# Exchanging transposed blocks of an attention kernel through memory instead of between partitions

## The chip, the cores and the metric

The kernel runs on one core of a Trainium2 chip. The metric is the device time of one execution in microseconds (us). The engines are TensorE (PE in the profile, its weight loads PEld), VectorE (DVE), ScalarE (ACT), GpSimd (POOL) and SyncE (SP), which here only issues transfers. Sixteen DMA engines carry them out. A tile lies in SBUF over 128 partitions.

## What is computed

The input x is (4, 128, 32, 32): four batches, 128 channels, 1024 positions. Cut to what matters, the reference is:

```python
N = H * W                                             # 1024
xg = x.reshape(B, 4, C // 4, H, W)                     # four groups of channels
y = (xg - mu) * rsqrt(var + EPS) * gn_gamma + gn_beta
q, k, v = split(einsum('bchw,dc->bdhw', y, w_qkv) + b_qkv, 3, axis=1)
scores = einsum('bnc,bcm->bnm', q, k) * C ** (-0.5)
w = softmax(scores, axis=-1)
a = einsum('bnm,bmc->bnc', w, v)
out = einsum('bchw,dc->bdhw', a, w_out) + b_out
return x + out
```

Everything is float32.

## The kernel before, in words

The two projections of queries and keys are folded into one matrix, and so are those of the values and of the output: per batch there is y (normalised input), z (y times the folded matrix) and v (values, the output matrix already in them). The scores are z times y, held in pairs of a head and a tail part (hi, lo) and multiplied in three passes.

The queries are worked in 32 blocks of 128, n = 0 to 31, eight per batch. One step of the program (a slot) handles one block on each engine. Four blocks are a group: eight groups, 0 to 7, of 512 queries each. For a block the order is: TensorE writes its scores (128 queries by 1024 keys, lines 778 to 781) two slots ahead; VectorE takes the maximum (line 577); ScalarE the exponential into `probs`, a ring of four blocks (line 426); then the block must be transposed, since the product with the values sums over the keys, which must lie on the partitions.

Group 0 and the last group are transposed on TensorE (`turn`, line 798). For groups 1 to 6 (`SWAPPED`) this is done in two steps. VectorE transposes within squares of 32 by 32 (`flip(n)`, line 605), issued one slot ahead of its block. A square is then right in itself but sits on the wrong 32 partitions. SyncE exchanges the squares (`swap(group)`, line 255) when all four blocks of the group are flipped: 16 transfers of 32 partitions by 4 KB, each from `flipped` on partitions 32g to `home` on partitions 32t. There are two tiles `flipped` and two `home`, used by even and odd groups in turn.

TensorE multiplies the home of a group with the values (`mix`, line 833), eight key tiles k of two passes each. The table `MIX` sets when: two tiles in each of the slots 4 group + 7 to 4 group + 10, that is, from four slots after the last flip of the group has been issued. Group 6 gets two tiles in slot 31 and the other six after the loop, then the last group follows. Before the first tile TensorE waits for all transfers of the group. VectorE then scales the product by the inverse row sums (`scale`, line 615), GpSimd adds the input (line 333), SyncE stores the result (line 265).

SyncE issues in the order of its program, one queue for all: for a group its inverse row sums to memory (`keep_rows`, line 238), the 16 swaps, the sums back, spread over all partitions (`spread_rows` into `inv_wide`, line 245), and the result of two groups before. Its waits hold all that stands behind them. A flip of groups 3 to 6 waits for the swaps of two groups before; a swap of these groups waits for the mix of two groups before.

Which transfer waits for which is said in its first lines:

```python
def swap(group):
    sp.wait_ge(s_flipped, QB * group)
    if group > 2:
        sp.wait_ge(s_mixed, KT * (group - 1))
```

Of the kernel before, what the change touches and what calls it, by code (L numbers as in the profile page):

```python
# [5 lines left out]
def attention_kernel(nc, x, vectors, weights, out):  # L6
# [36 lines left out]
    GROUP = QB * N  # L43
    GROUPS_OF_FOUR = BATCHES * HALVES
# [3 lines left out]
    SWAP = 16 * SQ * SQ  # L48
# [4 lines left out]

    inverse_rows = nc.dram_tensor("inverse_rows", (GROUPS_OF_FOUR - 1, HALF), fp32)

# [4 lines left out]
    with ctx:  # L60
        def sb(name, shape, dt=fp32):
            return ctx.enter_context(nc.sbuf_tensor(name, shape, dt))
# [58 lines left out]
        flipped_even = sb("flipped_even", [128, GROUP])  # L121
        with nc.sbuf_tensor("flipped_odd", [128, GROUP], fp32) as flipped_odd:
            pass
        last_head = sb("last_turned_head", [128, KT, HALF], fp32r)
        flipped = (flipped_even, flipped_odd)
        home = sb("home_even", [128, GROUP]), sb("home_odd", [128, GROUP])
# [63 lines left out]
        s_swapped = [sem("squares_swapped_even"), sem("squares_swapped_odd")]  # L190
# [24 lines left out]
        def swaps(group):  # L215

            return SWAP * len([g for g in SWAPPED if g <= group and g % 2 == group % 2])

# [8 lines left out]
        def _(sp):  # L227
# [20 lines left out]
            def swap(group):  # L248
                sp.wait_ge(s_flipped, QB * group)
                if group > 2:  # L250
                    sp.wait_ge(s_mixed, KT * (group - 1))
                for k in range(SQ):
                    for g in (0, 2, 1, 3):
                        t = g ^ k
                        sp.dma_start(home[group % 2][32 * t:32 * t + 32, g * N:(g + 1) * N],  # L255
                                     flipped[group % 2][32 * g:32 * g + 32, t * N:(t + 1) * N]
                                     ).then_inc(s_swapped[group % 2], 16)
# [11 lines left out]
            for group in SWAPPED:  # L269
                keep_rows(group)  # L270
                swap(group)
                spread_rows(group)
                if group >= 2:
                    store(group - 2)
# [114 lines left out]
        def _(act):  # L389
# [39 lines left out]
            def turned_copy(n):  # L429
                act.wait_ge(s_turned, 2 * turns(n) + 1)  # L430
                if n < QB:
                    act.activation(copy_of_turned(first_turned, n, 0), turned_tiles(0), ACT.Copy).then_inc(s_copied[0], 1)
                    return
                act.wait_ge(s_swapped[1], swaps(5))
                for j in range(2):
                    act.wait_ge(s_turned, 2 * turns(n) + j + 1)
                    act.activation(copy_of_turned(last_head, n, j), turned_tiles(j), ACT.Copy).then_inc(s_turned_hi, 1)
# [55 lines left out]
        def _(dve):  # L493
# [106 lines left out]
            def flip(n):  # L600
                group, u = n // QB, n % QB
                dve.wait_ge(s_exp, n + 1)
                if group > 2:
                    dve.wait_ge(s_swapped[group % 2], swaps(group - 2))
                dve.transpose(flipped[group % 2][:, :].rearrange("p (tv u c) -> p tv u c", u=QB, c=32)[:, :, u, :],  # L605
                              probs[:, n % RING, :].rearrange("p (v t r) -> p t v r", t=SQ, r=32)
                              ).then_inc(s_flipped, 1)
# [99 lines left out]
        def _(pe):  # L707
# [96 lines left out]
            def mix(group, count):  # L804
                b, g = group // HALVES, group % HALVES
                bank = mixed[:, g, :]
                for k in range(tiles_mixed[group], tiles_mixed[group] + count):
                    if k == 0:
# [11 lines left out]
                        if group in SWAPPED:  # L820
                            pe.wait_ge(s_swapped[g], swaps(group))
# [9 lines left out]
                    else:  # L831
                        there = home[g][:, :].rearrange("p (g v u c) -> p v u g c", g=SQ, v=KT, u=QB)[:, k, :, :, :]
# [120 lines left out]
```

## Time and profile before

| | us |
|---|---|
| median of 3 runs | 137.71 (137.03 to 138.33) |
| the profiled execution | 138.07 |
| its span in the profile | 136.3 |
| TensorE busy | 129.4 (95%) |
| VectorE busy | 99.8 (73%) |
| ScalarE busy | 65.0 (48%) |
| GpSimd busy | 41.4 (30%) |

The busy shares say which engine has room. The waits name who stood idle until whom. The chain follows what ended last back to its causes. A timeline lists instructions with their start and duration; for a transfer that is the time that SyncE took to issue it, and its landing is shown apart. A window's row gives for a stretch the busy time of each engine, the granted TensorE clock as a share of full speed, the mean busy share of the DMA engines and their GB/s.

### The profile page before, as it was taken

Reading aid. Unit: us, or ns where it says so; the run is one execution under the profiler, and the core shown is the slowest. Engines: PE = TensorE matmul, PEld = TensorE weight load, DVE = VectorE, ACT = ScalarE, POOL = GpSimd, SP = SyncE. Lnnn points to the kernel's source line nnn. Section 1 sums busy time; section 2 is a strip of 40 time slices with the busy share of each in tenths; the row PEclk is TensorE's granted clock in tenths of the full one; section 3 lists DMA queues with packets and bytes.
Section 4 is the critical chain, followed back from the end, with each engine's and each line's share of the span. In section 5 each row is a group of like instructions: output and inputs, shape, how many; then the busy total and the mean of one; then the engine's idle time right before and its main releaser. Section 6 shows DMA issues by size and latency. Waiting matters only on the chain.

```text
span 136.3 us, 1759 instructions
## 1 busy us (share of the span) xinstructions
PE 129.4 (95%) x543; PEld 89.1 (65%) x543; DVE 99.8 (73%) x170; ACT 65.0 (48%) x117; POOL 41.4 (30%) x49
## 2 busy tenths in 40 slices
PE   6999999998999949999999999999999999999990
PEld 6987688875777526666666666666656577554670
DVE  0589699999998996877686889866868886761302
ACT  3154778854675372544542475544633474730000
POOL 6032130730022229300190058000770367303210
PEclk9999999999999999999999999999999999999999
DMA  4940000030056978985689656888888459961011
GB/s 152 350 191 0 0 5 0 3 77 0 0 111 147 210 188 236 207 203 169 154 204 206 204 114 160 191 195 224 203 202 201 122 123 209 209 176 77 0 77 77
DMA packets 8937, 19.01 MB, mean 139 GB/s; under 512 B 3040, under 2 KB 3040, under 8 KB 8928
## 3 DMA queue, kind: packets, MB, share of 16 engines
q1 hardware_dynamic: 8640, 18.63, 53.8%
q10 hardware_dynamic: 288, 0.27, 0.6%
q8 instruction: 4, 0.07, 0.2%
q14 instruction: 5, 0.04, 0.2%
HBM read 4.20 MB, written 2.11 MB: 46 GB/s over the span
## 4 chain that ended last, share of the span: by engine, by line
PE 75%; DVE 12%; SPq 7%; issue 2%; DMA 2%; DVEq 0%
PE mixed L833 31%; PE scores L778 7%; SPq L255 7%; PE scores L779 7%; PE scores L781 7%; DVE scores L577 5%; PE scores L839 4%; PE turned L798 3%; DVE flipped_odd L605 3%; PE turned L723 3%; DMA home_odd<-flipped_odd 2%; PE mixed L830 1%; PE mixed L828 1%; PE mixed L829 1%; PE mixed L723 1%
## 5 line engine op out<-in xcount | busy, mean ns | idle before, releaser
L577 DVE TENSOR_SCALAR_CACHE_REDUCE scores<-scores,key_bias 128x1024 f32<-128x1024 f32 x31 | 40.0, 1289 | 15.0 <-PE scores L781 14.7
L426 ACT ACTIVATE probs<-scores,neg_max 128x1024 f32<-128x1024 f32 x32 | 35.7, 1116 | 22.7 <-DVE scores L577 21.9
L833 PE MATMUL mixed<-home_odd,v 128*128 128x512 f32 x48 | 22.6, 594 | 1.9 <-DMA home_odd<-flipped_odd 1.9
L833 PE MATMUL mixed<-home_even,v 128*128 128x512 f32 x48 | 22.1, 594 | 0.0
L778 PE MATMUL scores<-y_hi_odd,z_hi_odd 128*128 128x512 f32 x32 | 18.7, 585 | 0.6 <-DVE z_lo_odd L544 0.6
L778 PE MATMUL scores<-y_hi_even,z_hi_even 128*128 128x512 f32 x30 | 15.9, 531 | 0.0
L605 DVE STREAM_TRANSPOSE flipped_odd<-probs 128x1024 f32<-128x1024 f32 x12 | 14.8, 1235 | 0.3 <-DMA home_odd<-flipped_odd 0.3
L605 DVE STREAM_TRANSPOSE flipped_even<-probs 128x1024 f32<-128x1024 f32 x12 | 14.8, 1234 | 0.0
L833 PEld LDWEIGHTS mixed<-home_even,v 128*128 128x128 f32 x48 | 8.9, 189 | 7.8 <-issue 7.2
L833 PEld LDWEIGHTS mixed<-home_odd,v 128*128 128x128 f32 x48 | 8.5, 190 | 8.3 <-issue 8.0
L779 PE MATMUL scores<-y_lo_odd,z_hi_odd 128*128 128x512 f32 x32 | 12.6, 392 | 0.0
L333 POOL TENSOR_TENSOR result<-result,xs 128x512 f32<-128x512 f32 x7 | 8.9, 1278 | 9.9 <-DVE result L615 9.9
L779 PE MATMUL scores<-y_lo_even,z_hi_even 128*128 128x512 f32 x30 | 11.8, 392 | 0.0
L615 DVE TENSOR_TENSOR result<-mixed,inv_wide 128x512 f32<-128x512 f32 x7 | 7.4, 1051 | 4.4 <-PE mixed L833 4.4
L781 PE MATMUL scores<-y_hi_odd,z_lo_odd 128*128 128x512 f32 x32 | 9.9, 391 | 0.0
L778 PEld LDWEIGHTS scores<-y_hi_odd,z_hi_odd 128*128 128x128 f32 x32 | 6.0, 189 | 5.7 <-issue 3.6
L310 POOL TENSOR_TENSOR z_lo_odd<-z_full,z_hi_odd 128x512 fp32r<-128x512 f32 x2 | 2.6, 1300 | 22.3 <-ACT z_full L417 22.3
L781 PE MATMUL scores<-y_hi_even,z_lo_even 128*128 128x512 f32 x30 | 9.3, 392 | 0.0
L305 POOL TENSOR_TENSOR y_lo_odd<-y,y_hi_odd 128x512 fp32r<-128x512 f32 x4 | 5.1, 1289 | 13.6 <-ACT y_hi_odd L395 13.6
L779 PEld LDWEIGHTS scores<-y_lo_odd,z_hi_odd 128*128 128x128 f32 x32 | 6.0, 189 | 4.3 <-issue 3.6
L798 PEld LDWEIGHTS turned<-ident,probs 128*128 128x128 f32 x64 | 7.5, 140 | 1.9 <-issue 1.1
L798 PE MATMUL turned<-ident,probs 128*128 128x128 f32 x64 | 8.3, 272 | 0.0
(162 smaller groups left out, 202.9 us busy)
## 6 DMA issues: line engine op xcount, KB each, us to landing
home_odd<-flipped_odd SPq DMA_DIRECT2D x48, 128.0 KB, 2.4
home_even<-flipped_even SPq DMA_DIRECT2D x48, 128.0 KB, 2.4
out_dram<-result SPq DMA_DIRECT2D x8, 256.0 KB, 3.5
inv_wide<-inverse_rows SPq DMA_DIRECT2D x7, 256.0 KB, 3.6
xs<-in_x_dram SPq DMA_DIRECT2D x2, 512.0 KB, 6.5
xs<-in_x_dram SPq DMA_DIRECT2D x3, 256.0 KB, 4.6
xs<-in_x_dram ACTq DMA_DIRECT2D x1, 256.0 KB, 3.3
ws<-in_weights_dram SPq DMA_DIRECT2D x1, 256.0 KB, 4.0
```

The source lines that it names most:

```text
L255: sp.dma_start(home[group % 2][32 * t:32 * t + 32, g * N:(g + 1) * N], flipped[group % 2][32 * g:32 * g + 32, t * N:(t + 1) * N]).then_inc ...
L333: pool.tensor_tensor(result[:, g, :], result[:, g, :], xs[:, b, g * HALF:(g + 1) * HALF], ALU.add).then_inc(s_result, 1)
L426: act.activation(probs[:, i % RING, :], scores[:, i % 2, :], ACT.Exp, bias=neg_max[:, i:i + 1], scale=-1.0, accum_out=row_sum[:, i:i + 1]) ...
L577: dve.tensor_scalar(scores[:, i % 2, :], scores[:, i % 2, :], key_bias[:, b % 2, i:i + 1], None, ALU.subtract, ALU.min, accum_out=neg_max[ ...
L605: dve.transpose(flipped[group % 2][:, :].rearrange("p (tv u c) -> p tv u c", u=QB, c=32)[:, :, u, :], probs[:, n % RING, :].rearrange("p ( ...
L615: dve.tensor_tensor(result[:, g, :].rearrange("p (u q) -> p u q", u=QB), mixed[:, g, :].rearrange("p (u q) -> p u q", u=QB), inv_wide[:, g ...
L723: mm = pe.matmul(bank[:, (t - lo) * VW:(t - lo) * VW + C + 1], y[:, b % 2, t * 128:(t + 1) * 128], wv_out[:, 0:C + 1], start=True, stop=True)
L778: pe.matmul(to[h], z_hi[b % 2][:, query], y_hi[b % 2][:, halves[h]], start=True, stop=False)
L779: pe.matmul(to[h], z_hi[b % 2][:, query], y_lo[b % 2][:, halves[h]], start=False, stop=False)
L781: mm = pe.matmul(to[h], z_lo[b % 2][:, query], y_hi[b % 2][:, halves[h]], start=False, stop=True)
L798: mm = pe.transpose(turned[:, j, k * 128:(k + 1) * 128], probs[:, n % RING, key:key + 128], ident[:, :])
L833: mm = pe.matmul(bank, v[:, b % 2, k, :], there, start=first, stop=final)
```

## The change

A flipped block no longer goes from partitions to partitions. Each is written to a tensor in memory as soon as it is flipped (`keep`, 512 KB, 128 partitions with four pieces of 1 KB each), and two blocks at a time are read back to their home by four transfers (`bring`, each 256 KB: 32 partitions with four pieces of 2 KB). `flipped` becomes a ring of four blocks, laid out block by block, so the flip writes a contiguous row; `home` becomes three tiles, and the mix reads it in a new order of dimensions. A flip waits for the keep of the block four before (with its partner in the pair); a bring waits for the keeps of its two blocks and, from group 4 on, for the mix of three groups before. The head of the last group's turned blocks takes the place of `home_1` instead of `flipped_odd`, and its copy waits for the mix of groups up to 4.

```diff
-    SWAP = 16 * SQ * SQ
+    SQUARES = 32 * KT
+    HOMES = 3
+    SWAP = 16 * SQ * 2
...
+    squares = nc.dram_tensor("squares", (len(SWAPPED), 2, 128, SQ, 2, SQUARES), fp32)
...
-        flipped_even = sb("flipped_even", [128, GROUP])
-        with nc.sbuf_tensor("flipped_odd", [128, GROUP], fp32) as flipped_odd:
+        flipped = sb("flipped", [128, RING, N])
+        with nc.sbuf_tensor("last_turned_head", [128, KT, HALF], fp32r) as last_head:
             pass
-        last_head = sb("last_turned_head", [128, KT, HALF], fp32r)
-        flipped = (flipped_even, flipped_odd)
-        home = sb("home_even", [128, GROUP]), sb("home_odd", [128, GROUP])
+        home_1 = sb("home_1", [128, GROUP])
+        home = sb("home_0", [128, GROUP]), home_1, sb("home_2", [128, GROUP])
...
+        def pairs_kept(n):
+
+            return 32 * (n // 2 - 1)
...
-            def swap(group):
-                sp.wait_ge(s_flipped, QB * group)
-                if group > 2:
-                    sp.wait_ge(s_mixed, KT * (group - 1))
-                for k in range(SQ):
-                    for g in (0, 2, 1, 3):
-                        t = g ^ k
-                        sp.dma_start(home[group % 2][32 * t:32 * t + 32, g * N:(g + 1) * N],
-                                     flipped[group % 2][32 * g:32 * g + 32, t * N:(t + 1) * N]
-                                     ).then_inc(s_swapped[group % 2], 16)
+            def keep(n):
+                group, u = n // QB, n % QB
+                sp.wait_ge(s_flipped, n - QB + 1)
+                sp.dma_start(squares[group - 1, u // 2, :, :, u % 2, :],
+                             flipped[:, n % RING, :].rearrange("p (t w) -> p t w", t=SQ)).then_inc(s_kept, 16)
+
+            def bring(group, half):
+                sp.wait_ge(s_kept, pairs_kept(QB * group + 2 * half))
+                if half == 0 and group > HOMES:
+                    sp.wait_ge(s_mixed, KT * (group - HOMES + 1))
+                for t in range(SQ):
+                    there = home[group % HOMES][32 * t:32 * t + 32, :].rearrange("p (g w) -> p g w", g=SQ)
+                    sp.dma_start(there[:, :, half * 2 * SQUARES:(half + 1) * 2 * SQUARES],
+                                 squares[group - 1, half, :, t, :, :].rearrange("(g r) u w -> r g (u w)", g=SQ)
+                                 ).then_inc(s_swapped[group % HOMES], 16)
...
             for group in SWAPPED:
+                keep(QB * group)
+                keep(QB * group + 1)
+                bring(group, 0)
+                keep(QB * group + 2)
                 keep_rows(group)
-                swap(group)
+                keep(QB * group + 3)
+                bring(group, 1)
                 spread_rows(group)
...
-                if group > 2:
-                    dve.wait_ge(s_swapped[group % 2], swaps(group - 2))
-                dve.transpose(flipped[group % 2][:, :].rearrange("p (tv u c) -> p tv u c", u=QB, c=32)[:, :, u, :],
+                if group > SWAPPED[0]:
+                    dve.wait_ge(s_kept, pairs_kept(n - RING))
+                dve.transpose(flipped[:, n % RING, :].rearrange("p (t v c) -> p t v c", t=SQ, c=32),
...
-                        there = home[g][:, :].rearrange("p (g v u c) -> p v u g c", g=SQ, v=KT, u=QB)[:, k, :, :, :]
+                        there = home[group % HOMES][:, :].rearrange("p (g u v c) -> p v u g c", g=SQ, u=QB, v=KT)[:, k, :, :, :]
```

The queue of SyncE for group 3 before: its row sums, the 16 swaps, the sums back, the result of group 1.

```order
L238 DMA inverse_rows<-inv_sum 128x4 [waits group_inv_sums_ready]
L255 DMA home_odd<-flipped_odd 32x1024 [waits mixed_tiles_done,squares_flipped]
L255 DMA home_odd<-flipped_odd 32x1024 x15
L245 DMA inv_wide<-inverse_rows 128x512 [waits mixed_scaled,inv_rows_kept_odd]
L265 DMA out_dram<-result 128x512 [waits result_ready]
```

The same place after the change (its own line numbers: 258 is `keep`, 267 is `bring`, 252 and 277 the two old transfers).

```order
L258 DMA squares<-flipped 512x1x256 [waits squares_flipped] x2
L267 DMA home<-squares 32x4x512 [waits squares_kept]
L267 DMA home<-squares 32x4x512 x3
L258 DMA squares<-flipped 512x1x256 [waits squares_flipped]
L245 DMA inverse_rows<-inv_sum 128x4 [waits group_inv_sums_ready]
L258 DMA squares<-flipped 512x1x256 [waits squares_flipped]
L267 DMA home<-squares 32x4x512 [waits squares_kept]
L267 DMA home<-squares 32x4x512 x3
L252 DMA inv_wide<-inverse_rows 128x512 [waits mixed_scaled,inv_rows_kept_odd]
L277 DMA out_dram<-result 128x512 [waits result_ready]
```

One wait in front of 16 transfers has become two waits for landings, each with four brings behind it, and the third and fourth keep of a group stand behind the first half's brings.

VectorE around the first flips of group 3 before (577 is the maximum, 615 the scaling).

```order
L577 TENSOR_SCALAR scores,neg_max<-scores,key_bias 128x1024 [waits scores_ready,key_bias_ready]
L605 STREAM_TRANSPOSE flipped_odd<-probs 128x32x32 [waits squares_swapped_odd,exp_ready]
L615 TENSOR_TENSOR result<-mixed,inv_wide 128x512 [waits inv_spread_even,mixed_tiles_done]
L577 TENSOR_SCALAR scores,neg_max<-scores,key_bias 128x1024 [waits scores_ready,key_bias_ready]
L605 STREAM_TRANSPOSE flipped_odd<-probs 128x32x32 [waits squares_swapped_odd,exp_ready]
```

And after (594 is the maximum, 622 the flip, 632 the scaling).

```order
L594 TENSOR_SCALAR scores,neg_max<-scores,key_bias 128x1024 [waits scores_ready,key_bias_ready]
L622 STREAM_TRANSPOSE flipped<-probs 128x1024 [waits squares_kept,exp_ready]
L632 TENSOR_TENSOR result<-mixed,inv_wide 128x512 [waits inv_spread_even,mixed_tiles_done]
L594 TENSOR_SCALAR scores,neg_max<-scores,key_bias 128x1024 [waits scores_ready,key_bias_ready]
L622 STREAM_TRANSPOSE flipped<-probs 128x1024 [waits squares_kept,exp_ready]
```

No instruction of VectorE has moved; what a flip waits for is now a keep of the same ring of four, and this from group 2 on.

## Rows read from the trace of the kernel before

**Rows 1.** The page: span, and busy us of TensorE.

```profile
span 136.3 us, 1759 instructions
...
PE 129.4 (95%) x543; PEld 89.1 (65%) x543; DVE 99.8 (73%) x170; ACT 65.0 (48%) x117; POOL 41.4 (30%) x49
```

**Rows 2.** Waits: engine, line, waited for: us in total, times, longest.

```profile
DVE scores L577 <- PE scores L781: 14.7, 20, 1.3
...
PE mixed L833 <- DMA home_odd<-flipped_odd: 1.9, 1, 1.9
...
DVE flipped_odd L605 <- DMA home_odd<-flipped_odd: 0.3, 1, 0.3
...
SPq L251 <- PE mixed L833: 1.1, 2, 0.5
```

**Rows 3.** The chain from 33 to 58 us: start, us, what.

```profile
37.95 0.60 SPq L255
...
48.52 2.34 DMA home_odd<-flipped_odd
50.86 0.14 issue
51.00 1.96 PE mixed L833 x4
```

**Rows 4.** SP's timeline (start, us to issue), then landings of inv_wide.

```profile
26.98 0.32 SPq L245 DMA_DIRECT2D inv_wide<-inverse_rows  x1
...
64.55 10.04 SPq L255 DMA_DIRECT2D home_odd<-flipped_odd  x16
...
106.92 11.51 SPq L255 DMA_DIRECT2D home_even<-flipped_even  x16
...
DMA to landing us min/median/max: 3.4/3.6/4.6
```

**Rows 5.** TensorE's first mix tiles, groups 1, 2 and 6, and group 6 in the chain.

```profile
51.00 1.96 PE L833 MATMUL mixed<-home_odd,v 128*128 128x512 f32 x4 [1.85 <-DMA home_odd<-flipped_odd]
...
66.19 1.88 PE L833 MATMUL mixed<-home_even,v 128*128 128x512 f32 x4
...
120.36 7.11 PE L833 MATMUL mixed<-home_even,v 128*128 128x512 f32 x16
...
120.49 6.98 PE mixed L833 x16
```

**Rows 6.** Windows: busy us (count) by engine, clock, DMA share, GB/s; landing of swaps.

```profile
0.70:5.00 4.30, 3.96 (x18) 3.96 (x19) 1.40 (x3) 1.28 (x1) 2.25 (x11) 1.00 0.71 239
5.00:8.00 3.00, 3.00 (x24) 3.00 (x23) 1.27 (x6) 0.66 (x2) 0.76 (x2) 1.00 1.02 386
52.00:60.00 8.00, 8.00 (x33) 5.23 (x31) 6.02 (x9) 2.76 (x5) 3.37 (x3) 1.00 0.90 216
134.75:135.25 0.50, 0.00 (x0) 0.00 (x0) 0.00 (x0) 0.00 (x0) 0.00 (x0) 1.00 0.99 389
...
home_odd<-flipped_odd SPq DMA_DIRECT2D x48, 128.0 KB, 2.4
```

**Rows 7.** The results' stores (L265), and windows around the last one.

```profile
L265 SPq DMA_DIRECT2D out_dram<-result x8: 332/442/457, 61.0 to 133.8; - x8
...
DMA to landing us min/median/max: 2.0/3.5/3.7
...
134.50:134.75 0.25, 0.00 (x0) 0.00 (x0) 0.00 (x0) 0.00 (x0) 0.00 (x0) 1.00 0.48 188
...
135.25:135.50 0.25, 0.00 (x0) 0.00 (x0) 0.00 (x0) 0.00 (x0) 0.00 (x0) 1.00 0.23 82
```

**Rows 8.** Windows behind the first inv_wide.

```profile
27.50:28.50 1.00, 1.00 (x6) 0.80 (x6) 1.00 (x2) 1.00 (x2) 0.81 (x1) 1.00 0.00 0
28.50:29.00 0.50, 0.50 (x4) 0.26 (x2) 0.50 (x2) 0.45 (x3) 0.00 (x0) 1.00 0.17 37
```

**Rows 9.** VectorE's flips of blocks 5 and 7.

```profile
31.04 1.24 DVE L605 STREAM_TRANSPOSE flipped_odd<-probs 128x1024 f32<-128x1024 f32 x1
...
36.70 1.21 DVE L605 STREAM_TRANSPOSE flipped_odd<-probs 128x1024 f32<-128x1024 f32 x1
```

**Rows 10.** Windows at the end: the granted clock is third from last.

```profile
133.00:135.50 2.50, 0.02 (x1) 0.00 (x0) 0.69 (x1) 0.00 (x0) 0.00 (x0) 1.00 0.27 105
...
136.00:136.30 0.30, 0.00 (x0) 0.00 (x0) 0.00 (x0) 0.00 (x0) 0.00 (x0) 0.50 0.00 0
```

More of the change, by code:

```diff
@@ L189, in attention_kernel @@
         s_flipped = sem("squares_flipped")
-        s_swapped = [sem("squares_swapped_even"), sem("squares_swapped_odd")]
+        s_kept = sem("squares_kept")
+        s_swapped = [sem(f"squares_home_{k}") for k in range(HOMES)]
         s_mixed = sem("mixed_tiles_done")
@@ L215, in swaps @@
         def swaps(group):
-            return SWAP * len([g for g in SWAPPED if g <= group and g % 2 == group % 2])
+            return SWAP * len([g for g in SWAPPED if g <= group and g % HOMES == group % HOMES])
+        def pairs_kept(n):
+            return 32 * (n // 2 - 1)
         def copy_of_turned(to, n, j):
@@ L433, in turned_copy @@
                     return
-                act.wait_ge(s_swapped[1], swaps(5))
+                act.wait_ge(s_mixed, KT * 5)
                 for j in range(2):
@@ L820, in mix @@
                         if group in SWAPPED:
-                            pe.wait_ge(s_swapped[g], swaps(group))
+                            pe.wait_ge(s_swapped[group % HOMES], swaps(group))
                     if k % 4 == 0 and group not in SWAPPED:
```

## The prediction

> **What bounds the kernel now.** I read the busy shares first, then the waits, then the chain that ended last, then the SP queue in order of time, and last the DMA rates. TensorE is busy 129.4 of 136.3 us [rows 1]: nothing can be gained but its few holes. The waits show only one hole of TensorE that ends at a transfer, 1.9 us, and one of 0.3 us on VectorE [rows 2]; VectorE's 14.7 us behind the scores are the slack of the engine that is not the bound. The chain places the hole: the 16 swaps of group 1 go out from 37.95 to 49.1, the last lands 2.34 us after its issue began, and the mix of group 1 starts at 51.00 [rows 3]. Without that wait it would have started 1.85 us earlier, at 49.15. The later groups cause no wait: SP issues a group's swaps in 10 to 11.5 us, TensorE starts mixing a group every (120.36 - 51.00) / 5 = 13.87 us [rows 4, 5]. So the exchange has its own period, hidden below TensorE's, and what the change does to it is the question: a longer period costs nothing up to 13.87 us, and its excess in full, once per group, above that.
>
> The profiled execution took 138.07 us for a span of 136.3, 1.8 us around it; the median of the runs is 137.71, 0.4 us less.
>
> **What leaves.** 96 swaps of 128 KB, SBUF to SBUF, 2 MB a group. The hole of 1.85 us can go; behind it TensorE's own work is next, so that is the whole gain.
>
> **What comes, per group.** Four stores of 512 KB (keep) and eight loads of 256 KB (bring) through one queue: 4 MB where 2 MB went before. What sets the end is no longer only how much, but the order: SP keeps blocks 0 and 1, waits for both landings, brings half 0, keeps 2 and 3, waits, brings half 1. A bring cannot start before the landing, and the next keeps lie behind the bring in the queue. So the terms of a group add up, one behind the other:
>
> Keep: no row shows pieces of 1 KB. The nearest is the last store, 128 partitions in pieces of 2 KB, at 389 GB/s [rows 6]: 512 KB take 1.35 us, four 5.4 us. The other end is the rate of the swaps, 216 GB/s [rows 6]: 9.7 us. A gain below 5.4 has no room, since the loads on 128 partitions in 4 KB pieces ran at 386 GB/s with the DMA share at 1.02 [rows 6]. I take 5.4, the row that is nearest in kind.
>
> Bring: each one writes 32 partitions only. The loads that write 128 partitions ran at 386 GB/s, the swaps, which read 32 and write 32 partitions, at 216 GB/s with the engines 90% busy [rows 6]. So 32 partitions cost engine time, not idle time. Between 389 and 216 GB/s half a group (1 MB) takes 2.7 or 4.85 us. I take 4.85, since the share of 0.90 says that the engines were held up at the memory, and a bring has a side of the same 32 partitions. What I can't see is whether reading or writing was the slow side. Two halves: 9.7 us. The issues hide in it: four at 0.6 us [rows 3] are 2.4.
>
> The Trainium skill has a rule on this, and it speaks against the change: in SBUF — State Buffer, section Door 1: The DMA port swizzle (why `[64,N]` ≈ `[32,N]`), the rate goes by how many of 16 ports the partitions of one transfer reach, and partitions 0 to 31 reach eight. By that rule the swaps' row is a port limit and the bring inherits it; were the rule wrong for a one-sided transfer, the sum would be that of the first rival below. The page measures 189 GB/s for 1 MB into 32 partitions, an estimate of 5.5 us for a half where I take 4.85.
>
> Turning round: the last store is issued at 133.8 and landed 2.0 us later [rows 7], its bytes moved until some 135.3 (82 GB/s in the slice to 135.5, nothing behind it) [rows 7]: 0.5 us from last byte to landing, 0.8 us from issue to first byte. A load from memory takes longer to its first byte: the first inv_wide, issued at 26.98, shows nothing until 28.5 and then 37 GB/s in half a microsecond [rows 4, 8], so about 28.9: 1.9 us. Each half pays 0.5 + 1.9 = 2.4 us with the DMA engines empty, two 4.8 us. Bounds: 1.3 us (0.5 and a store's first byte) and 3.6 us, since the landings of inv_wide spread from 3.4 to 4.6 us [rows 4].
>
> The rest: one inv_wide and one store of 256 KB, 1.35 us at 389 GB/s.
>
> Sum: 5.4 + 9.7 + 4.8 + 1.35 = 21.25 us a group against TensorE's 13.87.
>
> **From the first group to the end.** The second flip ends at 31.04 + 1.24 = 32.3 [rows 9]. Its keep: 0.8 + 1.35 + 0.5, landed at 34.95. Bring 0 moves from 36.85 to 41.7, keeps 2 and 3 (flipped by 37.9) to 44.4, landed 44.9, bring 1 moves from 46.8 to 51.65, landed some 0.2 later: 51.85. TensorE could have begun at 49.15, so the removed hole comes back, 0.85 us longer. Group 2 has no store before it: 20.6 us. Four more at 21.25: the last byte of group 6 at 51.65 + 20.6 + 85 = 157.25, landed 157.45. Behind the first tile of group 6 the program has 136.3 - 120.49 = 15.8 us in the trace [rows 1, 5] (120.49 is its start in the chain, 120.36 in the timeline): 173.25, and 1.8 around it: 175.05.
>
> That the chain really runs free: when TensorE waits for group g, the two flips of the next group but one step are all that SP still needs, and they are done or depend only on keeps already sent. VectorE now waits in each flip from block 8 on, for the keep of four blocks before; behind it stand the maxima of two blocks on, then the exponentials and the scores. The keep of a group's third and fourth block lands some 15 us after the previous group's home is complete, so VectorE stands still for several microseconds, but the maximum it holds up feeds scores that TensorE reaches only after the mix that waits for the next home, at 21.25. No extra term. Behind SP's own waits stand the row sums' store, inv_wide and the result's store, which feed VectorE's scaling a group and more later.
>
> TensorE's clock: it is at full level throughout, falls to half only in the last 0.3 us [rows 10], some 3 us after the last matmul. Now TensorE stands 21.25 - 13.87 = 7.4 us idle a group, so it will fall to the 1.2 GHz level in those waits. In the groups the slack pays for it; in the last 12.5 us of matmuls it doesn't. Between nothing and 12.5 us (all at half); no row shows how soon it returns. In the first 5 us the first matmuls show clock 1.00 [rows 6], so I take 2 us, near the lower end. Total 177.
>
> Cost taken as nothing: the flips write one contiguous block, not 32-element pieces at four times the distance, some 1.24 us each as now [rows 9], hidden behind TensorE (24 of them; 0.1 us more each would hide in VectorE's 14.7). The mix reads its home in the same 32-element runs. The third home only removes waits on the mix of two groups before, which show 1.1 us in SP's waits [rows 2].
>
> **The rivals.**
> Full rate: a load into 32 partitions runs at 389 GB/s since only the reading side of the swaps was slow. For it: the swaps' landing stays at 2.4 us [rows 6], no backlog. Against: 90% busy engines. Half 2.7, group 5.4 + 5.4 + 4.8 + 1.35 = 16.95; group 1 complete at 47.55, in time; last landing 47.35 + 16.3 + 67.8 + 0.2 = 131.65; with 15.8 + 1.8 + 2: 151.
> Slow keeps: pieces of 1 KB go at the swaps' 216 GB/s. 2.43 instead of 1.35, 4.3 us more a group, 25 in all: 202. Against: the rows at 386 and 389 with 4 and 2 KB show no fall with the piece. The Trainium skill (DMA: Bandwidth & Descriptors, section Why small descriptors are slow (HBM only)) gives three cycles for each packet, which by my estimate is 3 in 35 for 1 KB: 0.1 us a keep, no rival by itself.
> Hidden round trips, the other side: the queue runs full rate and the turning round vanishes, because landings come while other bytes still move. Then a group is 12.15 us, and as long as each of the two turns costs less than (13.87 - 12.15) / 2 = 0.86 us the exchange stays under TensorE and only the hole goes: 138.07 - 1.85 = 136.2. It decides at 13.87 us a group. Against it: a landing alone took 0.5 and a first byte 0.8 us at the least, together 1.3.
>
> **How the numbers follow.** Forecast 0.62, full rate 0.18, slow keeps 0.12, hidden 0.04, something between, as a bring at 300 GB/s, 0.04. The forecast alone reaches from 169 (turns of 1.9 instead of 2.4 us, twelve of them, and no clock term) to 191 (turns of 3.6 us). The range takes in full rate with no clock term, 149, and part of the way to slow keeps: 148 to 192. About 1% is what a measurement of this kernel can tell from no change: faster by more 0.02, within 0.02, slower 0.96.
>
> **What would show it.** Right: SP's waits in front of the brings on the keeps, TensorE idle before the first mix tile of groups 2 to 6 by some 7 us each, these tiles 21 us apart, DMA at some 216 GB/s in the brings and near 389 in the keeps, VectorE idle before the flips, the clock below 1.00 in slices behind the waits. Group 1's mix at about 52. Full rate would show 17 us between the groups and over 350 GB/s in the brings; slow keeps 25 us. Wrong altogether: no wait of TensorE on the home, groups still 13.9 us apart.

## The result, and the profile after

The changed kernel takes 184.66 us (median of 4 runs, 184.58 to 184.79) against 137.84 us before (4 runs of the same comparison, 137.03 to 138.33): 1.3395 times, 95% interval 1.3355 to 1.3435. It is slower by 46.8 us. Forecast were 177, in a range of 148 to 192. Single executions can fall in a slower state of the chip, some per cent longer; times here go by the others, which leaves e1 with one of its two executions (173.05 us, the other 175.95).

The page of the changed kernel's profile: the span, busy us of each engine, and tenths of TensorE, clock and DMA over 40 slices.

```profile
span 182.9 us, 1738 instructions
...
PE 143.7 (79%) x543; PEld 94.1 (51%) x543; DVE 100.0 (55%) x170; ACT 65.2 (36%) x117; POOL 41.3 (23%) x49
...
PE   7999999899739997579907999177980799708992
...
PEclk9999999999975999879975999858999579975999
DMA  6800006397695939959499692995939969392011
```

Against [rows 1] no engine has more work, but TensorE has six holes, the clock falls in or just behind each, and the DMA line goes up and down in half groups. TensorE's busy time grew by 14.3 us without one more instruction: that is the lower clock. Some 12.6 us of it lie between groups 1 and 6, where TensorE had to wait for the homes anyway.

The waits, as in [rows 2] (us in total, times, longest):

```profile
DVE flipped L622 <- DMA squares<-flipped: 39.5, 9, 6.6
...
PE mixed L850 <- DMA home<-squares: 31.8, 6, 6.4
...
SPq L267 <- DMA squares<-flipped: 78.7, 12, 7.7
```

TensorE waits for a home in all six groups (before, in one), VectorE in nine flips, and SyncE stands 78.7 us in front of the twelve half-brings (line 267), each time for the landing of a keep (line 258). Three queues stop at one cause. SyncE's is the first of them: this is the row to read first.

The first mix tile of each group, to set against [rows 5] (start, us, and in brackets how long TensorE had waited):

```profile
53.45 3.75 PE L850 MATMUL mixed<-home,v 128*128 128x512 f32 x4 [4.51 <-DMA home<-squares]
...
75.31 2.38 PE L850 MATMUL mixed<-home,v 128*128 128x512 f32 x4 [3.53 <-DMA home<-squares]
...
97.27 3.61 PE L850 MATMUL mixed<-home,v 128*128 128x512 f32 x4 [5.98 <-DMA home<-squares]
...
120.20 3.75 PE L850 MATMUL mixed<-home,v 128*128 128x512 f32 x4 [5.27 <-DMA home<-squares]
...
143.06 3.75 PE L850 MATMUL mixed<-home,v 128*128 128x512 f32 x4 [6.44 <-DMA home<-squares]
...
165.13 8.96 PE L850 MATMUL mixed<-home,v 128*128 128x512 f32 x16 [6.11 <-DMA home<-squares]
```

The whole loss can be read from them. Group 1 starts at 53.45 instead of 51.00: 2.45 us. From there to group 6 are 111.7 us, 22.34 a group, instead of 69.4, 13.87 a group: 42.3 us. From group 6 to the end are 182.9 - 165.13 = 17.8 us instead of 15.9: 1.8 us, the clock (TensorE is busy 14.5 us there at a mean clock of 0.88, before 12.6 us at 0.99). Together 46.6, the difference of the spans.

SyncE's queue over three half-brings, to set against [rows 4] (start, us to issue):

```profile
124.29 1.98 SPq L267 DMA_DIRECT2D home<-squares  x4
126.33 0.52 SPq L258 DMA_DIRECT2D squares<-flipped  x1
126.90 0.62 SPq L245 DMA_DIRECT2D inverse_rows<-inv_sum  x1
127.56 1.12 SPq L258 DMA_DIRECT2D squares<-flipped  x1
135.35 1.73 SPq L267 DMA_DIRECT2D home<-squares  x4
137.18 0.38 SPq L252 DMA_DIRECT2D inv_wide<-inverse_rows  x1
137.60 0.43 SPq L277 DMA_DIRECT2D out_dram<-result  x1
138.07 1.27 SPq L258 DMA_DIRECT2D squares<-flipped  x2
146.78 1.75 SPq L267 DMA_DIRECT2D home<-squares  x4
```

Issuing takes about 4 us of the 11.1 and 11.4 between two half-brings; the rest is waiting for the last keep. A wait of SyncE for a landing with the DMA engines running dry around it is called a turn here: there are two in a group. Windows around the turns at 135.35 and 146.78 (the last three numbers are clock, DMA share, GB/s):

```profile
133.50:135.00 1.50, 1.50 (x6) 0.61 (x4) 0.00 (x0) 0.00 (x0) 0.00 (x0) 1.00 0.16 40
135.00:136.25 1.25, 1.25 (x7) 0.94 (x5) 0.82 (x1) 0.00 (x0) 0.00 (x0) 1.00 0.00 0
136.25:137.50 1.25, 0.37 (x2) 0.00 (x0) 1.25 (x2) 0.00 (x0) 0.00 (x0) 1.00 0.74 133
...
138.50:141.50 3.00, 0.00 (x0) 0.00 (x0) 2.89 (x5) 1.48 (x3) 1.12 (x1) 1.00 1.05 215
143.00:145.50 2.50, 2.44 (x3) 1.17 (x4) 0.00 (x0) 0.00 (x0) 1.51 (x2) 0.50 1.08 385
146.50:147.50 1.00, 1.00 (x4) 0.69 (x3) 0.00 (x0) 0.00 (x0) 0.00 (x0) 0.50 0.00 0
147.50:149.00 1.50, 1.50 (x7) 1.17 (x6) 0.00 (x0) 0.00 (x0) 0.00 (x0) 0.70 0.59 116
...
53.40:165.10 111.70, 82.03 (x264) 49.26 (x264) 55.46 (x82) 34.12 (x60) 24.39 (x20) 0.85 0.80 210
```

The brings run at 215 GB/s, the keeps at 385, both with the engines fully busy. A turn has three parts: the last bytes of the keeps come at a falling rate, then no byte moves for 1 to 1.25 us (2.0 us in one of the twelve turns), then the bring starts slowly, at 116 and 133 GB/s in the two turns shown. The first byte comes some 0.9 us after the bring's issue. TensorE's clock is at its lower level, 0.50, when its work comes back behind a wait of 4.5 us or more; behind the wait of 3.53 us it came back at 1.00 and fell 1.4 us later. The chain that ended last, followed as in [rows 3], goes from keep to bring or next keep in every half, with nothing of TensorE in it between 60 and 165 us:

```profile
70.92 8.03 DMA squares<-flipped
78.97 0.33 SPq L267
...
81.99 7.58 DMA squares<-flipped
...
92.88 8.06 DMA squares<-flipped
```

### The profile page after: what moved, and what is told of

Same layout as the page of the kernel before. It is cut to its first block, busy times and chain, and to the rows that moved or that the text cites. A ratio compares the mean times of both kernels' runs of the same rounds, so it can differ in the third digit from the quotient of the medians.

```text
span 182.9 us, 1738 instructions
## 1 busy us (share of the span) xinstructions
PE 143.7 (79%) x543; PEld 94.1 (51%) x543; DVE 100.0 (55%) x170; ACT 65.2 (36%) x117; POOL 41.3 (23%) x49
## 4 chain that ended last, share of the span: by engine, by line
DMA 52%; PE 18%; SPq 12%; DVE 9%; issue 6%; DVEq 0%
DMA squares<-flipped 48%; SPq L267 8%; PE mixed L850 5%; DVE scores L594 4%; DMA home<-squares 3%; PE scores L856 3%; DVE flipped L622 3%; SPq L245 2%; SPq L258 2%; PE mixed L847 1%; PE mixed L845 1%; PE mixed L846 1%; DVE first_turned L610 1%; PE scores L795 1%; PE scores L798 1%
## 5 line engine op out<-in xcount | busy, mean ns | idle before, releaser
L850 PE MATMUL mixed<-home,v 128*128 128x512 f32 x96 | 54.4, 701 | 31.8 <-DMA home<-squares 31.8
L622 DVE STREAM_TRANSPOSE flipped<-probs 128x1024 f32<-128x1024 f32 x24 | 29.7, 1236 | 39.5 <-DMA squares<-flipped 39.5
L850 PEld LDWEIGHTS mixed<-home,v 128*128 128x128 f32 x96 | 19.8, 220 | 50.8 <-issue 50.3
L795 PE MATMUL scores<-y_hi_odd,z_hi_odd 128*128 128x512 f32 x32 | 21.1, 659 | 0.6 <-DVE z_lo_odd L561 0.6
L795 PE MATMUL scores<-y_hi_even,z_hi_even 128*128 128x512 f32 x30 | 17.0, 568 | 0.0
L632 DVE TENSOR_TENSOR result<-mixed,inv_wide 128x512 f32<-128x512 f32 x7 | 7.2, 1032 | 12.5 <-PE mixed L850 12.5
L796 PE MATMUL scores<-y_lo_odd,z_hi_odd 128*128 128x512 f32 x32 | 13.7, 428 | 0.0
L798 PE MATMUL scores<-y_hi_odd,z_lo_odd 128*128 128x512 f32 x32 | 10.4, 408 | 0.0
L362 POOL TENSOR_SCALAR probs<-probs,inv_sum 128x1024 f32<-128x1024 f32 x4 | 4.5, 1122 | 19.8 <-DVE inv_sum L604 19.8
L454 ACT ACTIVATE last_turned_head<-turned 128x512 fp32r<-128x512 f32 x8 | 4.3, 595 | 11.4 <-PE turned L815 11.4
L419 ACT ACTIVATE v<-mixed 128x256 f32<-128x256 f32 (+1 forms) x5 | 2.0, 407 | 17.4 <-PE mixed L740 17.4
L843 PE MATMUL mixed<-first_turned,v 128*128 128x512 f32 x16 | 8.0, 592 | 0.0
```

Of the source, the lines that this page charges most:

```text
L622: dve.transpose(flipped[:, n % RING, :].rearrange("p (t v c) -> p t v c", t=SQ, c=32), probs[:, n % RING, :].rearrange("p (v t r) -> p t v ...
L632: dve.tensor_tensor(result[:, g, :].rearrange("p (u q) -> p u q", u=QB), mixed[:, g, :].rearrange("p (u q) -> p u q", u=QB), inv_wide[:, g ...
L795: pe.matmul(to[h], z_hi[b % 2][:, query], y_hi[b % 2][:, halves[h]], start=True, stop=False)
L796: pe.matmul(to[h], z_hi[b % 2][:, query], y_lo[b % 2][:, halves[h]], start=False, stop=False)
L798: mm = pe.matmul(to[h], z_lo[b % 2][:, query], y_hi[b % 2][:, halves[h]], start=False, stop=True)
L843: mm = pe.matmul(bank, v[:, 0, k, :], first_turned[:, k, :], start=first, stop=final)
```

## The experiments

"Time" is the median; the period is (start of group 6's mix less group 1's) / 5 in the profile. In e1, e3, e5, e8, e9 and e10 the brings carry other bytes than the exchange needs: these kernels leave it out and show only the time of the traffic.

| run | time, us | period, us |
|---|---|---|
| before | 137.6 to 138.5 | 13.87 |
| changed | 184.66 | 22.34 |
| e1, e5: brings fill 128 partitions | 173.05, 172.66 | 20.3, 20.0 |
| e2: turns hidden by order | 160.24 | 17.4 |
| e3: both | 141.47 | 14.6 |
| e8: no bring waits | 153.8 | 16.7 |
| e9: the same, 128 partitions | 143.91 | 15.4 |
| e10: e9 with eight flips, two homes | 143.29 | 15.3 |
| e4: eight flips, two homes | 185.24 | 22.1 |
| e6: brings alternate | 181.93 | 21.6 |
| e7: brings in two queues | 167.7 | 19.1 |
| w1: before, group 1 in halves | 142.85 | 14.3 |
| w2: before, squares that stay | 136.33 | 13.85 |

**The width of a bring.**

```diff
-                for t in range(SQ):
-                    there = home[group % HOMES][32 * t:32 * t + 32, :].rearrange("p (g w) -> p g w", g=SQ)
-                    sp.dma_start(there[:, :, half * 2 * SQUARES:(half + 1) * 2 * SQUARES],
-                                 squares[group - 1, half, :, t, :, :].rearrange("(g r) u w -> r g (u w)", g=SQ)
...
+                there = home[group % HOMES][:, :].rearrange("p (g w) -> p g w", g=SQ)
+                sp.dma_start(there[:, :, half * 2 * SQUARES:(half + 1) * 2 * SQUARES],
+                             squares[group - 1, half, :, :, :, :].rearrange("p t u w -> p t (u w)")
```

> Each half of a group comes back in one transfer of 1 MB into all 128 partitions (every partition its own row) instead of four of 256 KB into 32 partitions each; the same bytes, pieces of 2 KB as before. The exchange between partitions is left out by this, so the output is not the reference's. Theory (a transfer into 32 partitions runs at about 216 GB/s, one into 128 at about 389): each half gets 2.15 us shorter, the groups come 22.3 - 4.3 = 18.0 us apart, the time is 184.7 - 12 x 2.15 = 159 us. Rival (the brings are slow because they read from memory while it is also written, whatever partitions they fill): the rate stays near 216 GB/s, the time at 184 to 186. Rival (round trips are all that counts, the rate nothing): above 180.

Measured: 173.05 us. None of the three: some 12 us gained where 26 were expected. The groups are 20.3 us apart, not 18.0. Windows inside one of its first halves (bring issued at 97.10), rising rate, then the keeps:

```profile
98.50:100.00 1.50, 1.50 (x6) 0.91 (x5) 1.50 (x2) 0.00 (x0) 0.55 (x1) 1.00 0.78 115
100.00:102.00 2.00, 2.00 (x12) 1.45 (x11) 2.00 (x4) 1.33 (x3) 1.84 (x2) 1.00 1.05 340
103.00:105.00 2.00, 2.00 (x14) 1.74 (x13) 0.63 (x2) 1.20 (x2) 0.00 (x0) 1.00 1.10 377
```

A bring into 128 partitions does run faster than 215 GB/s, 340 once it flows, but it needs 1.5 us at 115 GB/s to get there. A half got 1.0 us shorter by it, not 2.15. To see whether the single large transfer is to blame, its half was cut in four again, each over 128 partitions (`home[...][:, t * N + ...]` from `squares[..., :, t, :, :]`).

> The changed kernel, each half brought back by four transfers of 256 KB that each fill all 128 partitions (one piece of 2 KB on each), where the wide bring of before used one of 1 MB; the exchange between partitions is left out, so the output is not the reference's. The wide bring in one piece gave 174.5, not 159. Theory A (one transfer of 512 pieces starts late, so the turn grew from 2.9 to 3.7 us): 162 to 168 us. Theory B (the slow start is the memory's, the first reads after an idle stretch; it costs more bytes at the full rate): 172 to 176 again. Theory C (only the number of transfers and their 32 partitions' descriptors count, not the rate): near 184.

Measured: 172.66 us (1.2542 times before, 1.2445 to 1.264). The number of theory B, at the lower edge of its band. The cut gave next to nothing, 0.4 us, and a slow start is there as well: 160 GB/s in the microsecond from 117.0, behind an issue at 116.07. So the size of the transfer is not to blame; that the memory is, as theory B has it, these rows don't show.

**The order of the four brings** (`for t in (0, 2, 1, 3)`).

> The changed kernel with the four brings of a half in the order of partitions 0, 64, 32, 96 instead of 0, 32, 64, 96. Everything is computed. Theory (all 16 engines work on one transfer at a time, in order, so neighbours in the queue don't share the time): 184.7 within 1.5. Rival (two neighbours on different halves of the partitions overlap): towards the 174.5 of the wide bring.

Measured: 181.93 us (1.3215 times before, 1.3102 to 1.3328), 2.7 us below the changed kernel and outside the 1.5 us of the theory, but far from the 174.5 that the rival named. The intervals just miss each other (1.3102 to 1.3328 and 1.3355 to 1.3435), and the groups are 21.6 us apart instead of 22.3: a small gain from alternating the halves of the partitions, whose cause stays open.

**The turns, by order.** SyncE's loop:

```diff
                 keep(QB * group)
                 keep(QB * group + 1)
-                bring(group, 0)
+                if group >= 2:
+                    bring(group - 1, 1)
+                    spread_rows(group - 1)
+                if group >= 3:
+                    store(group - 3)
                 keep(QB * group + 2)
                 keep_rows(group)
                 keep(QB * group + 3)
-                bring(group, 1)
-                spread_rows(group)
-                if group >= 2:
-                    store(group - 2)
+                bring(group, 0)
...
```

> Only SyncE's order is changed: the second half of a group is brought after the next group's first two keeps have been issued, the first half after its own third and fourth keep, so a bring waits for keeps that landed while other bytes moved (two counters for the keeps instead of one). Everything is computed. Theory (the two turns of a group cost some 2.9 us each with empty DMA engines, and add up with the bytes): groups 22.3 - 5.8 = 16.5 us apart, complete time 154 to 158 us. Rival (the DMA engines are the bound by their bytes, the turns lie beside them): within 3 us of 184.7. Rival (VectorE's waits in the flips set the pace): still over 175.

Measured: 160.24 us (1.1572, 1.1475 to 1.1669): 24.4 us gained by order alone, with every byte as before. The windows over its middle show DMA engines almost without gaps, and the waits show VectorE's standing in the flips down from 39.5 to 0.3 us:

```profile
53.00:143.00 90.00, 76.53 (x263) 47.27 (x264) 51.27 (x78) 33.02 (x58) 22.88 (x19) 0.91 0.99 256
```

```profile
DVE flipped L627 <- DMA squares<-flipped: 0.3, 1, 0.3
```

It stayed 2 us above the band. The second bring of a group now stands behind a keep whose flip VectorE can't reach while TensorE waits: SyncE's two keeps issued from 91.30 took 8.8 us, until the flip that began at 98.34 was nearly done. VectorE had waited 5.64 us for the scores in front of that flip, and these came behind the mix of 92.09, which had waited for its home. SyncE's waits name the flips (in the changed kernel 6.8 us):

```profile
SPq L259 <- DVE flipped L627: 41.4, 16, 9.8
```

**Both together.**

> The wide brings of the first experiment and the order of the second together (the exchange between partitions is left out, so the output is not the reference's). Theory: a group is then 5.4 + 5.4 + 1.35 = 12.2 us of bytes and no turns, below TensorE's 13.87 us, so all goes behind TensorE, and the hole before group 1's mix is gone as well: 136 to 137 us, the groups 13.9 apart, no wait of TensorE on a home. Rival (memory traffic of 4 MB a group has a cost of its own, in the flips or in TensorE's reading of the homes): over 142.

Measured: 141.47 us (1.0193, 1.0112 to 1.0273). Between the two forecasts: 18.8 us below e2, yet 3 us above before. TensorE still waits for three homes, 5.6 us in all:

```profile
PE mixed L854 <- DMA home<-squares: 5.6, 3, 2.3
```

The windows show the DMA engines full all the way:

```profile
50.00:120.00 70.00, 65.48 (x242) 41.59 (x243) 50.91 (x77) 32.02 (x58) 24.15 (x19) 1.00 1.01 310
```

**The turns, taken away.** The brings read the input x, so they need no landing (`wait_ge(s_kept, ...)` in `bring` has nothing left to guard; each pair of keeps has a counter of its own).

> The changed kernel with its own order; the brings read the input x (the same 2 MB a group, the same pieces, into the same partitions) instead of the kept squares, so they need not wait for a landing and none of them does; the squares are still kept, and a flip still waits for the keep four blocks before. The exchange is left out, so the output is not the reference's. Theory (the rate and the turns together made the 47 us, and the turns alone are some 2.9 us a half): a group is 5.4 + 9.7 + 1.35 = 16.5 us of bytes, group 1 is home in time at about 47, the time 148 to 152 us. Rival (the engines' bytes are the bound, the landing waits lie beside them): above 175. The order with hidden turns gave 160.2 because its second bring waits for flips that TensorE's own wait holds up; this one has no such tie.

Measured: 153.8 us (1.1163, 1.1102 to 1.1224), 1.8 us above the band: group 1 was not home at 47, its mix began at 52.26. The period is 16.66 us against 16.45 worked out. The brings from x run at the rate of those from the kept squares:

```profile
47.00:51.00 4.00, 2.55 (x9) 1.32 (x7) 3.96 (x9) 1.17 (x3) 1.20 (x1) 1.00 1.05 215
```

So the turns are worth 31 us, 5.7 us of each 22.3, and what is left is the moving of bytes. e2, which kept the same bytes and the same source, gained 24.4 us of them.

> The run before this one with brings that fill all 128 partitions (four of 256 KB a half, from x). The exchange is left out, so the output is not the reference's. Theory: 5.4 + 5.4 + 1.35 = 12.2 us of bytes a group, under TensorE's 13.87: no wait on a home at all, also not before group 1, 136 to 137 us. Rival (memory that is read and written at once gives less than 389 GB/s, as the wide bring's missing 15 us hint): a group of 14 to 16 us, 140 to 148 us.

Measured: 143.91 us (1.0452, 1.0389 to 1.0515): the number of the rival. Not 12.2 us a group but 15.4. The windows over the same stretch without and with wide brings, the first of e8, then of e9:

```profile
53.00:125.00 72.00, 63.53 (x221) 39.81 (x220) 47.08 (x68) 27.82 (x51) 19.43 (x16) 0.95 1.04 280
```

```profile
49.00:125.70 76.70, 71.34 (x264) 44.84 (x262) 55.53 (x84) 36.59 (x65) 25.27 (x20) 0.98 1.02 300
```

The engines are full in both, and move 280 and 300 GB/s. For e8 that is the sum of a 389 and a 216 part: a group's 4.7 MB in 16.45 us are 287 GB/s. For e9 no such sum holds: parts at 385 and 340 GB/s would make 13 us a group, not 15.4. VectorE also waited 10.4 us in e9's flips, and TensorE only 1.1 us on a home; the ring of four could have been the cause.

> The run with wide brings and no turns (143.9 us), with room for eight flipped blocks and two homes. The exchange is left out, so the output is not the reference's. That run had the DMA engines fully busy from 49 to 125.7 us at 300 GB/s, and VectorE waited 10.4 us in the flips for keeps. Theory A (reading and writing memory in turn gives 300 GB/s and not 389: 4.7 MB a group take 15.7 us, over TensorE's 13.87, whoever waits): 141 to 145 us, the groups some 15.4 apart, TensorE now waiting on the homes instead of behind the flips. Theory B (the bytes fit, and the flips' wait for a ring of four costs the 7 us): 136 to 138 us.

Measured: 143.29 us (1.0404, 1.0321 to 1.0487): theory B falls, and the time is that of theory A. With room for eight flips the wait moved to where A put it, and nothing was won. That shows the full queue as the bound, not the reason that A gives for its rate. Its windows, then its waits:

```profile
49.00:125.00 76.00, 71.68 (x264) 45.09 (x263) 55.05 (x82) 36.03 (x63) 25.31 (x20) 0.98 1.03 303
```

```profile
PE mixed L850 <- DMA home_odd<-in_x_dram: 3.5, 2, 2.6
PE mixed L850 <- DMA home_even<-in_x_dram: 1.2, 2, 0.8
```

**The third home and the ring of four.**

```diff
-    HOMES = 3
+    HOMES = 2
...
-        flipped = sb("flipped", [128, RING, N])
+        flipped_even = sb("flipped_even", [128, RING, N])
...
+        flipped = flipped_even, sb("flipped_odd", [128, RING, N])
...
-                    dve.wait_ge(s_kept, pairs_kept(n - RING))
+                    dve.wait_ge(s_kept, pairs_kept(n - 2 * RING))
```

> The changed kernel with room for eight flipped blocks instead of four and two homes instead of three; a flip waits for the keep of eight blocks before, a bring for the mix of two groups before. Everything is computed. Theory (SyncE's chain of keeps, turns and brings runs free; the 39.5 us that VectorE waits in the flips lie beside it, and the third home is worth nothing): 184.7 within 1.5 us, with VectorE's wait on the keeps nearly gone. Rival (the ring of four makes VectorE late, which delays scores and keeps): faster by 5 us or more. Rival (the third home is needed): slower by 3 us or more.

Measured: 185.24 us (1.3377, 1.327 to 1.3483), no different from the changed kernel. VectorE's 39.5 us in the flips are gone from the waits, TensorE's 34.6 us on the homes are there as before (31.8). Two things changed at once, and one could hide the other; but in front of the brings SyncE's waits still name keeps alone, and no mix, for which a missing third home would make it wait:

```profile
SPq L267 <- DMA squares<-flipped_even: 41.6, 6, 7.3
SPq L267 <- DMA squares<-flipped_odd: 38.4, 6, 7.7
```

So a wait of 39.5 us was worth nothing, and neither was the third home.

**Two queues.** On e2, `bring` splits: t = 0, 1 from SyncE, t = 2, 3 from ScalarE, two of its slots per group.

> On the order with hidden turns (160.2 us): of each half's four brings two (partitions 0 to 63) go through SyncE's queue and two (64 to 127) through ScalarE's. Everything is computed. Theory (a queue is worked in order, but two queues are worked side by side, so both halves of the partitions are filled at once): the brings come near the full rate, the time near the 141.5 us of the wide brings, up to 145 with ScalarE's 24 issues of some 0.4 us. Rival (32 partitions per transfer halve the rate whatever else runs): 158 to 162. Rival (ScalarE's waits delay the exponentials): over 165.

Measured: 167.7 us (1.216, 1.2076 to 1.2243), 7.5 us slower than e2. The theory falls. In a half whose brings SyncE issued from 103.13 and ScalarE from 105.27, the rows show 164 and 206 GB/s, not above the 215 of one queue:

```profile
93.00:94.00 1.00, 0.01 (x1) 0.04 (x1) 0.00 (x0) 0.00 (x0) 1.00 (x2) 0.50 1.09 376
106.00:110.00 4.00, 4.00 (x19) 2.74 (x18) 2.77 (x6) 2.24 (x5) 0.00 (x0) 1.00 0.91 164
110.00:112.00 2.00, 1.99 (x9) 1.30 (x7) 0.85 (x3) 0.25 (x2) 0.00 (x0) 1.00 1.07 206
```

The row at 376 is of a stretch with keeps in it. 167.7 us lie where the last rival put the time, over 165. Whether the brings' own rate made it longer than e2's, or ScalarE's coming some 2 us late with its half of them or standing in front of them, these rows don't tell; it stays open.

**A version below both.** The profile of before has one hole that ends at a transfer, 1.85 us before group 1's mix [rows 5]. The first try split that group's exchange:

```diff
+            sp.wait_ge(s_flipped, 2)
+            exchange(1, 0, 2)
+            sp.wait_ge(s_flipped, 4)
+            exchange(1, 2, 4)
             for group in SWAPPED:
...
```

> The kernel before with the block-by-block layout of the change (flipped and home by t or g, block, key tile), everything else as before but for group 1: its first two blocks are swapped between partitions as soon as they are flipped (16 transfers of 64 KB), the other two after (16 more). Everything is computed. Theory (the only hole that the exchange makes is the 1.85 us before group 1's mix, and its half can go out 5.6 us earlier): issues of 0.43 to 0.5 us, the last landing at 49 to 50 instead of 50.86, time 0.8 to 1.8 us below before, 136.0 to 137.0. Rival (32 issues take longer than the 16 did and the last landing comes no earlier): within 0.5 us of before.

Measured: 142.85 us (1.0387, 1.0323 to 1.0451), slower; worse than the rival. SyncE's timeline has the reason:

```profile
31.92 20.51 SPq L260 DMA_DIRECT2D home_odd<-flipped_odd  x30
```

Thirty issues in 20.5 us are 0.68 each; a swap of 64 KB costs SyncE what one of 128 KB does (median 0.59). TensorE waited 6.5 us instead of 1.9. So fewer transfers, not smaller ones: four of the sixteen squares stay on their partitions and need none.

```diff
-                for k in range(SQ):
+                for k in range(1 if group == 1 else 0, SQ):
...
+                        for t in range(SQ):
+                            pool.wait_ge(s_stayed, t)
+                            part = slice(32 * t, 32 * t + 32), slice(t * N, (t + 1) * N)
+                            pool.tensor_copy(home[1][part], flipped[1][part]).then_inc(s_stayed, 1)
```

> The kernel before; for group 1 alone the four squares that stay on their partitions (t = g) are copied from flipped to home by GpSimd, and SyncE issues the other twelve swaps. Everything is computed. Theory (the splitting in halves failed since a swap costs SyncE 0.64 us whatever its size, 32 of them 20.5 us; four issues less end 2.5 us earlier): the last landing at 48.4 or before, TensorE's hole of 1.85 us gone, time 1.4 to 1.9 us below before. Rival (GpSimd's four copies of 1.1 us and more are done later than the swaps, after 49): less than 0.5 us gained, or slower, with TensorE waiting for GpSimd.

Measured: 136.33 us against 137.62 in the same comparison, 0.9888 times, 0.986 to 0.9915. The gain is 1.3 us, about 1%, small but outside the interval of no change; the mechanism is the one expected, the size a little less. Swaps and copies lie side by side, and in its waits TensorE has none on a home any more (the first mix begins at 49.44, not 51.00):

```profile
38.36 7.59 SPq L256 DMA_DIRECT2D home_odd<-flipped_odd  x12
...
38.40 4.32 POOL L375 COPY home_odd<-flipped_odd 32x1024 f32<-32x1024 f32 x4 [9.69 <-DVE flipped_odd L616]
```

## Why the prediction was right, point by point

It said slower, by one chain: keep, landing, bring, keep, landing, bring, its period above TensorE's. That chain is what the profile shows and what e2 and e8 take apart. One term of the sum came out near by luck. The terms of the sum:

- Keep, 389 GB/s: 385 measured. Pieces of 1 KB cost nothing over 2 KB; the rival of slow keeps is out.
- Bring, 216 GB/s: 215 measured, the engines at 1.05. The choice between 2.7 and 4.85 us was right for this kernel. Its reason was half right: a swap is also paced by its issue (0.64 us for 64 KB and for 128 KB alike), 128 KB in 0.64 us are 205 GB/s, so the row of the swaps had two limits at about the same place. It is e1 that ties the rate to the width, 215 against 340 GB/s. The rule of the Trainium skill that was weighed (SBUF — State Buffer, section Door 1: The DMA port swizzle) fits these two numbers; no run here tests its ports by themselves.
- Turning round, 2.4 us a half: the term that was mis-sized. Measured are (22.34 - 16.45) / 2 = 2.95 us, by e8 directly (22.34 - 16.66) / 2 = 2.84. It came that near by two errors that partly cancel. The prediction took the turn as 2.4 us without a byte, 1.9 of them from a bring's issue to its first byte, after inv_wide. Measured are some 0.9 us, close to the 0.8 us of the store that it kept for its lower bound, and without a byte 1 to 1.25 us in eleven of twelve turns. The rest of the loss stands on both sides of that: the keeps' last bytes at a falling rate (40 GB/s over 1.5 us at 133.50) and the bring's slow start (133 GB/s over 1.25 us at 136.25). The prediction had neither. Of the 7.7 us that the forecast fell short, 1.6 are in group 1 (53.45 instead of 51.85), and 6.1 in the five periods (111.7 instead of 105.6), of which ten turns of 0.55 more make 5.5.
- "The chain really runs free", VectorE's waits worth nothing: right, by e4. TensorE's idle time was foreseen as some 7 us a group; it waited 3.5 to 6.4 us, since the lower clock stretched its work by 12.6 us over the five periods.
- The clock, 2 us at the end: 17.8 instead of 15.9 us, 1.8. No row stood behind the 2 us, a choice near the lower end of nothing to 12.5, so this is luck.

The Full rate rival named the right doubt and gave it too much. With 128 partitions it would have been 151 (159 with the 7.7 us by which the forecast fell short); e1 and e5 gave 173.1 and 172.7. Both it and the rival of hidden round trips worked with 389 GB/s for everything. e9 and e10 show that a group's traffic in this order, without a bring that waits for a landing, takes 15.3 to 15.4 us at 300 to 303 GB/s; in e3's order it took 14.6. All lie above 13.87, so the rival of hidden round trips, too, had a group's 12.15 us too low: of the forms tried here none came below before, and the best of them, e3, is 2% above it without making the exchange; the best that makes it, e2, is 16% above.

By parts: of the 46.8 us the turns are 31 (184.7 to 153.8, e8), the width then 10 (153.8 to 143.9, e9), and the last 6 are left by a queue that is full and still takes longer than TensorE. The width alone gives some 12 us while the turns are there (e1, e5), and 18.8 once order hides them (e2 to e3).

What stays open: why a full queue of keeps and wide brings moves 300 to 310 GB/s where its parts show 385 and 340. That it comes from writing and reading the memory in turn is a guess that was not tried by itself.

## What to carry to other kernels

A round trip through memory is priced as a chain and not as bytes: here each wait for a landing cost some 2.9 us of DMA engines running dry, empty or starting, two of them a group beside 16.5 us of bytes. If it must be made, put other transfers between a write and the read that waits for it, so that its landing passes under their bytes; order alone gave 24 of 47 us back. And where many waits appear at once, look first at that of the issuing queue: here it was the cause, and removing 39.5 us of VectorE's waits changed nothing.

## What the runs showed that was not expected

- SyncE needs 0.59 us and a gap of 0.04 for a transfer between partitions, for 64 KB (w1) as for 128 KB (before), but 0.43 us for one of 256 KB from memory with four times the pieces (the changed kernel).
- DMA engines at a share of 0.99 to 1.08 moved 215, 256, 280, 300 and 385 GB/s in these runs (a bring, e2, e8, e9, the keeps): their busy share alone says nothing of the rate.
- Two issuing queues brought no more than one: 164 and 206 GB/s in e7, against 215.
- The lower clock of TensorE, 0.50 behind the waits, cost 12.6 us of longer matmuls between groups 1 and 6 (82.03 busy instead of 69.4). The chain that ended last has nothing of TensorE in it between 60 and 165 us, so it cost nothing visible there; the 1.8 us of the end counted.
